# Inverse standard deviations of two layer norms: VectorE bit estimate and Newton steps in place of ScalarE's square root, in a two-layer graph network kernel

## What is computed

```python
o1 = (adj == 1) @ (x @ w1); o2 = (adj == 2) @ (x @ w2); o3 = (adj == 3) @ (x @ w3)
x = layernorm(x + o1 + o2 + o3 + bias)            # (x - mean) / sqrt(var + 1e-5)
h = x @ W.T + b
e = leaky_relu(h @ we1 + be1 + (h @ we2 + be2).T)
x = layernorm(x + softmax(where(adj > 0, e, -9e15)) @ h)
```

## Time and profile before

| what | value |
|---|---|
| median of 3 runs | 1558.68 us (1557.68 to 1558.89) |
| the profiled execution, device time | 1559.72 us |
| its span, first to last instruction | 1558.1 us |
| TensorE matmul busy | 1422.6 us (91%) |
| VectorE busy | 1092.0 us (70%), 2432 instructions |
| ScalarE busy | 978.1 us (63%), 1534 instructions |
| mean granted TensorE clock | 0.976 |

### The profile page before, as it was taken

One profiled execution on the slowest core, in us unless ns is written; L12 is line 12 of the kernel. 1 busy time (PEld: TensorE's weight loads), 2 busy tenths in 40 slices (PEclk: granted clock), 3 DMA queues, 4 the chain that ended last, 5 costly groups with the idle time before them and its releaser, 6 DMA issues. The chain is left out here.

```text
span 1558.1 us, 19404 instructions
## 1 busy us (share of the span) xinstructions
PE 1422.6 (91%) x6934; PEld 670.4 (43%) x6934; DVE 1092.0 (70%) x2432; ACT 978.1 (63%) x1534; POOL 116.1 (7%) x154
## 2 busy tenths in 40 slices
PE   0867697989999999999999987999999999999996
PEld 0433243444444444444444433444444444444443
DVE  3677667877877868768778657576667676666663
ACT  1333526457457556456456559787888788788873
POOL 2111011100110100100100021000000000000000
PEclk9999799999999999999999997999999999999998
DMA  9999999993979979967969311000000000100100
GB/s 133 138 126 116 126 110 119 128 114 49 117 96 99 106 69 123 83 68 96 84 67 119 28 62 47 8 28 28 28 28 28 28 28 28 55 28 28 35 1 15
DMA packets 87684, 109.60 MB, mean 70 GB/s; under 512 B 4960, under 2 KB 71072, under 8 KB 87584
## 3 DMA queue, kind: packets, MB, share of 16 engines
q0 software_dynamic: 67584, 67.12, 47.1%
q1 hardware_dynamic: 20000, 41.20, 8.0%
HBM read 296.49 MB, written 13.14 MB: 199 GB/s over the span
## 5 line engine op out<-in xcount | busy, mean ns | idle before, releaser
L1222 PE MATMUL ps<-pos_masks,tables 128*128 128x512 fp8e4 x2048 | 616.4, 383 | 39.2 <-DVE pos_masks L607 32.1
L1004 ACT ACTIVATE neg_masks<-e_row,cols 128x512 int8<-128x512 f32 x816 | 509.7, 708 | 110.9 <-PE ps L1222 46.3
L1222 PE MATMUL ps<-neg_masks,tables 128*128 128x512 fp8e4 x1632 | 492.1, 383 | 0.0
L1180 PE MATMUL ps<-edge_masks,tables 128*128 128x512 fp8e4 (+1 forms) x2048 | 464.1, 385 | 0.0
L1222 PEld LDWEIGHTS ps<-pos_masks,tables 128*128 128x128 f16 x2048 | 200.4, 99 | 285.9 <-issue 49.5
L1180 PEld LDWEIGHTS ps<-edge_masks,tables 128*128 128x128 f16 x2048 | 201.4, 99 | 233.3 <-issue 13.7
L1222 PEld LDWEIGHTS ps<-neg_masks,tables 128*128 128x128 f16 x1632 | 161.3, 99 | 197.7 <-issue 9.0
L605 DVE TENSOR_TENSOR neg_masks<-pos_masks,neg_masks 128x2048 uint16<-128x2048 uint16 x102 | 125.0, 1225 | 91.4 <-ACT neg_masks L1004 88.3
L589 DVE TENSOR_SCALAR edge_masks<-edges 128x512 uint16<-128x512 uint16 x512 | 123.4, 306 | 78.1 <-PE ps L1180 78.1
L589 DVE TENSOR_SCALAR pos_masks<-edges 128x512 uint16<-128x512 uint16 x512 | 114.2, 285 | 88.4 <-PE ps L1222 88.4
L992 ACT ACTIVATE edges<-ps 128x1024 uint8<-128x1024 bf16 x64 | 65.1, 1017 | 172.5 <-PE ps L1189 172.5
(11 more groups left out here) (133 smaller groups left out, 845.0 us busy)
## 6 DMA issues: line engine op xcount, KB each, us to landing
adj_in<-adj POOLq DMA_DIRECT2D x84, 512.0 KB, 12.2
tables<-adj POOLq DMA_DIRECT2D x28, 512.0 KB, 31.2
e_row<-e_scratch SPq DMA_DIRECT2D x34, 256.0 KB, 3.9
edges<-adj POOLq DMA_DIRECT2D x16, 512.0 KB, 11.9
part_scratch<-a_c_rows SPq DMA_DIRECT2D x18, 256.0 KB, 2.5
part_in<-part_scratch SPq DMA_DIRECT2D x18, 256.0 KB, 3.0
edges<-x SPq DMA_DIRECT2D x8, 512.0 KB, 6.6
x_rows<-x SPq DMA_DIRECT2D x8, 512.0 KB, 5.5
```

What stands on the lines that cost most here:

```text
L1004: ins = e.activation(gate_bufs[GATE[m]][:, n:n + GR].bitcast(I8), e1row[:, q % 2, :], ACT.Sign, bias=t2[:, JC * c + j:JC * c + j + 1])
L1180: ins = e.matmul(ps[:, h, :], v_hl[:, i, JC * c + j, :], U0[:, n:n + GR].bitcast(kind), start=c == 0 and j == 0 and i == 0, stop=c == NCH ...
L1222: ins = e.matmul(z_bank(q, k), tab[:, c, 2 * k + i, j, :], mask[:, n:n + GR].bitcast(F8A), start=first and j == 0 and i == 0, stop=final a ...
```

## The change

The square root on ScalarE and the reciprocal on VectorE go, in both layer norms. In their place VectorE runs `rsqrt`, 11 small instructions, each of which waits for the one before: a shift right by one of the variance's bits, minus that plus the constant 0x5f3759df as the first value y, and three rounds of t = y*y, t = -0.5*t*v, y = (t + 1.5)*y. It stands inside `statistics` and `statistics2`, right behind the addition of EPS, and the product with minus the mean follows it at once. `sd_of` and `sd2_of` are gone from ScalarE's order, and the products with minus the mean, which stood in `rs_of` and `rs2_of` (at E+7), are made at E+5. ScalarE's `out_of` stands at E+6 instead of E+8, and `AFTER`, the number of steps behind the last batch, is 7 instead of 9.

```diff
-AFTER = 9
+AFTER = 7
+            def rsqrt(y, v, tmp, done, n):
+                e.tensor_scalar(tmp.bitcast(I32), v.bitcast(I32), 1, None, ALU.logical_shift_right).then_inc(done, 1)
+                e.wait_ge(done, RSQ * n + 1)
+                e.tensor_scalar(y.bitcast(I32), tmp.bitcast(I32), -1, ROOT, ALU.mult, ALU.add).then_inc(done, 1)
+                for i in range(3):
+                    e.wait_ge(done, RSQ * n + 3 * i + 2)
+                    e.tensor_tensor(tmp, y, y, ALU.mult).then_inc(done, 1)
+                    e.wait_ge(done, RSQ * n + 3 * i + 3)
+                    e.scalar_tensor_tensor(tmp, tmp, -0.5, v, ALU.mult, ALU.mult).then_inc(done, 1)
+                    e.wait_ge(done, RSQ * n + 3 * i + 4)
+                    e.scalar_tensor_tensor(y, tmp, 1.5, y, ALU.add, ALU.mult).then_inc(done, 1)
             def statistics(S):
...
                 e.tensor_scalar(var0[:, :], mv0[:, :, 1], EPS, None, ALU.add).then_inc(s_var, 1)
-            def rs_of(S):
-                e.wait_ge(s_sd, S + 1)
-                e.reciprocal(rs0[:, :], sd0[:, :]).then_inc(s_rs, 1)
-                e.wait_ge(s_rs, S + 1)
+                e.wait_ge(s_var, S + 1)
+                rsqrt(rs0[:, :], var0[:, :], sd0[:, :], s_rs, S)
+                e.wait_ge(s_rs, RSQ * (S + 1))
                 e.scalar_tensor_tensor(nm0[:, :], mv0[:, :, 0], -1.0, rs0[:, :], ALU.mult, ALU.mult).then_inc(s_nm, 1)
...
                 e.tensor_scalar(var2[:, :], mv2[:, :, 1], EPS, None, ALU.add).then_inc(s_var2, 1)
-            def rs2_of(f):
-                e.wait_ge(s_sd2, f + 1)
+                e.wait_ge(s_var2, f + 1)
                 ge(e, s_out, f)
-                e.reciprocal(rs2[:, :], sd2[:, :]).then_inc(s_rs2, 1)
-                e.wait_ge(s_rs2, f + 1)
+                rsqrt(rs2[:, :], var2[:, :], sd2[:, :], s_rs2, f)
+                e.wait_ge(s_rs2, RSQ * (f + 1))
                 e.scalar_tensor_tensor(nm2[:, :], mv2[:, :, 0], -1.0, rs2[:, :], ALU.mult, ALU.mult).then_inc(s_nm2, 1)
...
-                for q in ended(m - 7):
-                    if q >= LOWS:
-                        rs2_of(q - LOWS)
...
-                    if off == 2:
-                        rs_of(S)
...
-            def sd_of(S):
-                e.wait_ge(s_var, S + 1)
-                e.activation(sd0[:, :], var0[:, :], ACT.Sqrt).then_inc(s_sd, 1)
...
-            def sd2_of(f):
-                e.wait_ge(s_var2, f + 1)
-                e.activation(sd2[:, :], var2[:, :], ACT.Sqrt).then_inc(s_sd2, 1)
...
                 for q in ended(m - 6):
-                    if q >= LOWS:
-                        sd2_of(q - LOWS)
-                for q in ended(m - 8):
                     if q >= LOWS:
                         out_of(q - LOWS)
...
-                for S, off in tails(k):
-                    if off == 2:
-                        sd_of(S)
```

More of the change, by code:

```diff
@@ L51 @@
 EPS = 1e-5
+RSQ = 11
+ROOT = 0x5f3759df
 NO_EDGE = -9e15
@@ L266, in build @@
             "edge_masks_ready", "layer0_multiplied")
-        s_y, s_xg, s_xb, s_o, s_v, s_st, s_mv, s_var, s_sd, s_rs, s_nm, s_x1 = sems(
+        s_y, s_xg, s_xb, s_o, s_v, s_st, s_mv, s_var, s_rs, s_nm, s_x1 = sems(
             "y_ready", "xg_in", "xb_ready", "o_ready", "v_ready", "stats_ready", "mean_ready", "var_ready",
-            "sd_ready", "rs_ready", "minus_mean_ready", "x1_ready")
+            "rs_ready", "minus_mean_ready", "x1_ready")
         s_x1st, s_pe, s_er, s_e1c, s_e1T, s_e1Tc, s_e1st, s_bd = sems(
@@ L284, in build @@
         s_x1i = [sem(f"x1_in_{n}") for n in range(2)]
-        s_proj, s_zr, s_num, s_rd, s_v2, s_st2, s_mv2, s_var2, s_sd2, s_rs2, s_nm2, s_out = sems(
+        s_proj, s_zr, s_num, s_rd, s_v2, s_st2, s_mv2, s_var2, s_rs2, s_nm2, s_out = sems(
             "projected", "empty_rows", "numerators", "reciprocals", "v2_ready", "stats2_ready", "mean2_ready",
-            "var2_ready", "sd2_ready", "rs2_ready", "minus_mean2_ready", "out_ready")
+            "var2_ready", "rs2_ready", "minus_mean2_ready", "out_ready")
         s_store = [sem(f"out_stored_{n}") for n in range(2)]
```

## The result

The kernel with the change takes 1588.35 us (median of 6 runs, 1586.41 to 1590.86), the kernel before takes 1558.79 beside it (1557.33 to 1559.80). The ratio is 1.019, with an interval of 1.0178 to 1.0202: 29.6 us slower, where the forecast was 28.9.

A forecast was written before the change was run, and what follows sets the result against it. TensorE ends last almost everywhere; in four-batch sweeps VectorE's chain from collect to masks has no slack. 12.9 (sweeps) + 10.2 (clock) + 4.0 (tails) + 1.8 (drain) = 28.9 us on 1558.68 gives 1587.6 us, range 1573 to 1599.

The forecast's parts named there:

- The late chain: Eight four-batch sweeps, VectorE from collect to masks: 2.4 us added each, 19.2, less 6.3 from ScalarE, +12.9 us.
- The clock: TensorE at 1.2 GHz behind six of eight lengthened idle times, 1.7 us each: +10.2 us, bounds 0 and 13.6.
- second rival: VectorE's chain as forecast, but TensorE's clock stays at 2.4 GHz: 1577 us, chance 18%.
- ScalarE's credit: Four-batch stretch: ScalarE gets back only its lateness, 0.9 us in each of seven cycles, 6.3 us.
- The first rival: ScalarE matters: stretch falls to TensorE's floor, 9.5 us goes at tails of blocks 0 to 3; 1537 us, 7%.
- The rsqrt step: Each of VectorE's eleven dependent small instructions takes 0.20 us from start to start, 2.2 us together.
- third and fourth rival: Third: VectorE overlaps the steps, no change, 1559, 5%. Fourth: table loads stay or 0.3 us a step, 1597, 10%.
- The tails: Ends of layer 1's row blocks: ScalarE's wait goes, VectorE has 2.0 us more; +4.0 us, bounds -4 and +9.
- TensorE has a queue of ready work: Tails of blocks 3 to 6: TensorE only 2.2 us idle in 500, so cost 0.
- The drain: Behind the last batch, var to output grows from 0.85 to 2.6 us: +1.8 us, with nothing beside it.
- the long step: Upper bound for VectorE's eleven instructions: 2.5 us in place of 2.2.

The follow-up runs named there:

- l1_sqrt: The changed kernel with layer 1's inverse roots as before (square root on ScalarE, reciprocal on VectorE): 1583.13 us, ratio 1.0153 to the kernel before.
- l1_behind: The changed kernel with layer 1's eleven steps and product later in the slot, behind its second masks: 1586.95 us, ratio 1.0181 to the kernel before.
- l1_one_round: The changed kernel with one Newton step in place of three in layer 1 alone: 1582.70 us, ratio 1.0158 to the kernel before.
- stats_moved: The changed kernel with layer 2's statistics at E+6 in place of E+5 where the next sweep has four batches: 1549.93 us, ratio 0.9948.
- best: stats_moved with layer 1's square root back on ScalarE, placed behind `convert`: 1546.64 us, ratio 0.9920 to the kernel before.
- out_late: stats_moved with ScalarE's output back at E+8, where the kernel before has it: 1551.73 us, ratio 0.9947 to the kernel before.
- dummy_sqrt: stats_moved with square roots of constants on ScalarE at E+6, read by nobody, bringing table loads back: 1552.14 us, ratio 0.9949 to the kernel before.
- one_round: The changed kernel with one Newton step in place of three in layer 2 alone: 1569.45 us, ratio 1.0069 to the kernel before.
- five_rounds: The changed kernel with five Newton steps in place of three in layer 2 alone: 1604.39 us, ratio 1.0291 to the kernel before.
- l2_sqrt: The kernel before with layer 1 alone changed to VectorE's eleven steps: 1564.90 us, ratio 1.0045 to the kernel before.
- before_moved: The kernel before with layer 2's statistics one batch later where the next sweep has four, roots staying on ScalarE: 1581.79 us, ratio 1.0144.

## Why the prediction was right, and where not

**The late chain: right.** The eight sweeps were to cost 12.9 us and the clock 10.2, 23.1 in all; measured are 22.8. The first of them grew by 2.38 us (10.25 from 7.87). The seven cycles took 231.5 us; less the five falls of the clock in them, at 1.7 each, that is 31.9 us a cycle, the forecast's number. The two cycles without a fall, such as the one from 1302.51 to 1334.38, took 31.87 each. What carried it was one reading: `collect` waits for TensorE, TensorE waits for the masks, so what lies between has no slack, whatever the shares say.

**The clock: right in number, six of eight, and partly by luck.** The six was a choice between none and eight, and nothing in the trace of before said which. In three other kernels with the same idle times of 3.19 us it was six (l1_sqrt), six (l1_behind) and five (l1_one_round) of eight. The second rival (clock up, 1577) fell with the batches of 8.75 us.

**ScalarE's credit: right as a limit.** ScalarE never waits for a broadcast row in the stretch any more, and it got no more than its lateness: the first of the seven cycles before, from 1225.32 to 1254.80 us, took 29.48 us, which is VectorE's 29.5, and the later ones 29.8 to 31.7.

**The first rival had the mechanism.** The chain decides at 6.92 us. With 7.45 and 2.4 it was on the wrong side; stats_moved, at 6.07, is on the other, and there the stretch fell to TensorE's floor as that rival says. Of its 9.5 us at the tails none came that the runs can tell, in best: the transposes' wait for the root is followed by one for VectorE.

**The rsqrt step: right.** 0.20 us, for the integer instructions as for the others; the third and fourth rival fell with it.

**The tails: mis-sized, 5.7 us measured, 4.0 forecast.** The lag of after behind before at the same place of both executions was 1.97 us ahead of block 0's tail, 0.92 behind it, 3.75 behind block 1's, 2.36 ahead of block 2's, 4.80 behind it, 7.97 from the end of block 3's tail to 918 us, and 7.70 behind block 7's. So block 0 gave 1.1 (forecast 1.2), block 1 cost 2.8 (1.7), block 2 2.4 (3.0), block 3 3.2 (0), block 7 gave 0.3 (0.5 forecast as a cost), and 1.4 came back between blocks 1 and 2. Block 1's wait in front of the attention terms, and block 3's in front of its transposes:

```profile
248.21 0.62 PE L1182 MATMUL ps<-idb,packed_bf 128*128 128x128 bf16 x8 [1.58 <-ACT packed_bf L990]
252.52 0.37 PE L1200 MATMUL ps<-idf,cols 128*8 128x128 f32 x1 [3.68 <-DVE cols L667]
...
520.97 0.62 PE L1182 MATMUL ps<-idb,packed_bf 128*128 128x128 bf16 x8 [2.25 <-ACT packed_bf L990]
```

The step that failed is "TensorE has a queue of ready work" for blocks 3 to 6. The trace of before had, for the transposes of the same piece in block 3, this row:

```profile
513.00 0.62 PE L1189 MATMUL ps<-idb,packed_bf 128*128 128x128 bf16 x8 [0.62 <-ACT packed_bf L983]
```

An idle time of 0.62 us is small, but it says that TensorE was waiting here on ScalarE, and by it on VectorE: `convert` in turn had waited 2.20 us for VectorE's packing. An idle time of 1.45 us stood three slots ahead of it in the same tail, at 469.32; the two slots between had none. The share of idle time (2.2 in 500) hid this. Only blocks 4 to 6 had the slack. Of the 1.4 us that came back, 1.1 did so at a broadcast row: at 334.15 before, TensorE waited 5.19 us for a `convert` that stands behind the row's sign masks, and the row took 4.5 us from issue to landing there and 3.5 in after, where the wait is 4.11. Why the row landed sooner isn't shown.

**The drain: its term right, its sum not.** var to output grew by 1.73 us (1.8 forecast), but the projection took 1.16 us of TensorE instead of 2.09, and from collect to its result it was 3.27 instead of 4.20 us. Net 0.6.

**What isn't the change's.** 2.5 of the 7.7 us ahead of the stretch stood there before the first matmul (30.11 instead of 27.59 us), in code that is the same; 0.5 of it was gone ahead of block 0's tail, so 2.0 of the 7.7 are not the tails'. The first batch of the stretch began anywhere from 1220.9 to 1227.7 us in the five kernels of the table that share the tails of the kernel with the change (stats_moved, out_late, dummy_sqrt, one_round, five_rounds). So single executions can't settle a term of 2 us there; the medians of l2_sqrt and l1_sqrt, 7 and 5.8 us for layer 1, fit the 5.7. The errors of the tails, of the drain and this start partly cancelled, and the close hit of the total is in part luck. That of the late stretch isn't, but for the number of falls.

**The range.** By the prediction's own terms its upper end adds up to 1598.7 us and not 1600 (1587.6, and 3.4 for the clock, 2.4 and 0.3 for the long step, 5 for the tails). The range given stops at 1599 all the same.

## What to carry to other kernels

An instruction added to an engine costs what its place costs: find the wait on both sides of that place first, and if the engine waits for its consumer ahead of the piece and the consumer for it behind, each microsecond counts in full, at any share of busy time. The way out is often to keep the work and move it by one step, to where the engine would wait anyway, but look on each other engine for who then waits for the moved result, and what is queued behind. A short idle time in front of a consumer (0.62 us here) meant that there was no slack, not that there was little to lose.

## What the hardware showed that I had not expected

- **The clock behind equal idle times.** TensorE's idle time of 3.18 or 3.19 us, the same batch ahead of each, brought the clock down to 1.2 GHz behind six of eight; 2.01 us (one_round) behind none of eight; 4.37 us (five_rounds) behind all eight, behind two for about twice as long. In the kernel before, 2.45 us brought it down and 2.57 us, at 1430.70, didn't. A fall cost 1.7 us in after, and 1.3 to 2.9 in five_rounds. Two windows of after, behind the first of them (granted 0.76) and at the one at 1302.51 (1.00):

```profile
1235.00:1242.00 7.00, 6.60 (x23) 2.70 (x24) 3.52 (x7) 7.00 (x12) 0.00 (x0) 0.76 0.43 124
1299.00:1306.00 7.00, 3.81 (x19) 1.62 (x18) 4.38 (x12) 6.93 (x13) 0.00 (x0) 1.00 0.47 150
```

- **A switch of tables without a drain.** In before_moved's rows above the signs end at 1281.62, the load starts at 1281.64 and the exponent follows at 1282.93: 1.3 us for a switch. The Trainium skill ("ScalarE: Activation LUTs", What ACT_TABLE_LOAD costs) has about 2.66 us; the load's 1283 ns agrees, a drain isn't seen on either side of it.
- **Integer steps cost what float steps do.** The shift and the integer multiply-add on 128 x 4 took 0.17 us each, 0.20 from start to start, as the float product does.
